# Four graph layers on one core: in layer 1, a constant one in the place of the last feature carries a term of the attention logits

## The reference

```python
x = layernorm(x + L0(x, adj))      # relational graph convolution
x = layernorm(x + L1(x, adj))      # the layer of this change
x = layernorm(x + L2(x, adj))      # attention with 8 heads
x = layernorm(x + L3(x, adj))      # graph attention with 8 heads

def L1(feat, adj):
    h = feat @ W
    Ax, Ay = h @ a_1, h @ a_2
    A_xy = (h @ a_12) @ h.T
    logits = Ax.T + Ay + A_xy
    e = where(adj > 0, leaky_relu(logits, 0.2), -9e15)
    h_prime = softmax(e) @ feat
    return elu(feat @ W_1 + h_prime @ W_2)
```

## Time and profile before

| | us |
|---|---|
| median of 3 runs | 802.0 |
| the 3 runs | 802.0, 802.37, 793.09 |
| the profiled execution, device time | 794.29 |
| its span, first to last instruction | 792.5 |
| mean granted TensorE clock | 0.976 of full |

### The profile page before, as it was taken

The page is one execution under the profiler, slowest core; times in us unless marked ns, Lnnn a source line. Parts: engine busy times, 40 slices in busy tenths (PEclk is TensorE's granted clock), DMA queues, the critical chain, the costliest instruction groups (busy, mean ns, idle before and its releaser), DMA issues.

```text
span 792.5 us, 17776 instructions
## 1 busy us (share of the span) xinstructions
PE 706.9 (89%) x6465; PEld 524.9 (66%) x6525; DVE 614.9 (78%) x1578; ACT 540.0 (68%) x933; POOL 449.6 (57%) x486
## 2 busy tenths in 40 slices
PE   3899599999678999999999999889999999999982
PEld 2777377777545666666666666667777777777761
DVE  3799648888846777878787878788888888888882
ACT  0545267777727666766666666558989898988882
POOL 5377403443334445665655566556666777677776
PEclk9999899999959999999999999999999999999997
DMA  8900000000000000000000000000000000000001
GB/s 239 247 2 1 1 1 1 2 1 2 1 0 1 2 1 2 1 2 2 1 2 1 2 1 2 2 2 1 15 15 14 15 29 15 14 16 19 24 14 41
DMA packets 28888, 14.94 MB, mean 19 GB/s; under 512 B 1920, under 2 KB 28800, under 8 KB 28800
## 3 DMA queue, kind: packets, MB, share of 16 engines
q1 hardware_dynamic: 25344, 12.59, 5.8%
q10 hardware_dynamic: 3456, 1.20, 0.7%
HBM read 9.59 MB, written 4.19 MB: 17 GB/s over the span
## 4 chain that ended last, share of the span: by engine, by line
PE 48%; issue 22%; POOL 12%; DVE 9%; POOLq 6%; ACT 2%; DVEq 0%; ACTq 0%
PE pair L954 18%; PE pair L1030 10%; POOL X L503 8%; POOLq L498 6%; PE pair L1055 4%; PE pair L1117 3%; DVE arena L932 2%; DVE nmx L938 2%; PE pair L1107 2%; PE pair L1093 2%; PE pair L1072 2%; PE pair L1104 2%; PE pair L1077 2%; PE pair L1086 2%; PE pair L1147 1%
## 5 line engine op out<-in xcount | busy, mean ns | idle before, releaser
L585 POOL TENSOR_TENSOR arena<-arena,nmx 128x1024 f32<-128x1024 f32 x64 | 121.4, 1897 | 116.2 <-DVE nmx L896 116.2
L599 POOL TENSOR_TENSOR arena<-arena,nmx 128x1024 f32<-128x1024 f32 x64 | 121.4, 1897 | 75.3 <-DVE nmx L938 75.1
L954 PE MATMUL pair<-identf,arena 128*128 128x128 f32 x1088 | 149.5, 279 | 2.5 <-ACT arena L732 2.1
L954 PEld LDWEIGHTS pair<-identf,arena 128*128 128x128 f32 x1088 | 117.5, 141 | 43.1 <-issue 38.9
L497 POOL TENSOR_TENSOR ln<-ln,neghalf 128x4 f32<-128x4 f32 x64 | 66.3, 1036 | 134.9 <-DVE ln L537 134.9
L503 POOL TENSOR_SCALAR X<-yb,ln 128x128 f32<-128x128 f32 x256 | 112.6, 453 | 11.9 <-issue 11.9
L888 DVE TENSOR_TENSOR arena<-pair,mask 128x1024 f32<-128x1024 f32 x64 | 78.4, 1225 | 51.8 <-PE pair L1030 51.7
L728 ACT COPY arena<-pair 128x1024 f32<-128x1024 f32 x64 | 64.8, 1012 | 74.0 <-PE pair L954 74.0
L1030 PE MATMUL pair<-arena,hg 32*128 32x256 f32 x512 | 91.1, 432 | 3.5 <-DVE arena L888 2.4
L757 ACT ACTIVATE arena<-pair 128x1024 f32<-128x1024 f32 x64 | 66.2, 1034 | 30.6 <-PE pair L1107 30.6
L896 DVE TENSOR_REDUCE nmx<-arena 128x8 f32<-128x1024 f32 x64 | 78.0, 1219 | 1.8
(11 more groups left out here) (169 smaller groups left out, 1405.0 us busy)
## 6 DMA issues: line engine op xcount, KB each, us to landing
X<-in_x SPq DMA_DIRECT2D x16, 256.0 KB, 6.0
arena<-in_adj SPq DMA_DIRECT2D x16, 256.0 KB, 6.2
out<-X SPq DMA_DIRECT2D x16, 256.0 KB, 2.3
nat_all<-in_L_gnn_W ACTq DMA_DIRECT2D x2, 64.0 KB, 4.5
w<-in_L_gnn_W ACTq DMA_DIRECT2D x2, 64.0 KB, 5.1
nat_all<-in_L_gnn_W_loop ACTq DMA_DIRECT2D x1, 64.0 KB, 2.7
nat_all<-in_L_gnn_Wg_loop ACTq DMA_DIRECT2D x1, 64.0 KB, 3.4
hg_bias<-in_L_gnn_b_loop ACTq DMA_DIRECT2D x1, 64.0 KB, 5.0
```

Source lines behind the costliest of these rows:

```text
L585: nc.gpsimd.tensor_tensor(v3(P2[t % 3], HEADS), v3(P2[t % 3], HEADS), nmx2[t % 2][:].unsqueeze(2).broadcast_to([128, HEADS, N]), ALU.add)\
L599: nc.gpsimd.tensor_tensor(v3(p, HEADS), v3(p, HEADS), nmx2[(t - 1) % 2][:].unsqueeze(2).broadcast_to([128, HEADS, N]), ALU.add)\
L954: last = nc.tensor.transpose(dst[:, cols(i)], src[:, cols(i)], identf[:])
```

## The change

On GpSimd a constant matrix `center` is set (the identity, with minus one in its last row, and a last column of zeros). On TensorE `w1T` is a matmul with `center` in place of a transpose, and two new products make `w12c` from `w12`. `bil` is made in two pieces: 127 columns as before, and a last column W times a_2, the vector that was spread into `wa2` before. `wa2` is gone. TensorE waits for `pool_ready` ahead of the products and no longer behind them. On VectorE two memsets, of 32 partitions by 512 columns each, write ones into the last partitions of both `xT` tiles ahead of layer 1; the copy to `xT` then writes 127 partitions, so that the last stays one. The first copy waits for the memsets. In each turn the four matmuls of line 1002 go, and `xw` uses `w12c`.

```diff
+        center = sb("center", [128, 128])
...
+        w12c = sb("w12c", [128, 2 * D])
...
-        wa2 = sb("wa2", [128, 128])
...
-        w1_at = add(w1T[:], nat["L1_gnn_W"])
+        w1_at = add(w1T[:], nat["L1_gnn_W"], center[:])
+        for half in range(2):
+            add(w12c[:, cols(half)], center[:], w12[:, cols(half)])
...
-        add(bil[:], w1T[:], a12w[:], a12w_at)
+        add(bil[:, 0:D - 1], w1T[:], a12w[:, 0:D - 1], a12w_at)
+        add(bil[:, D - 1:D], w1T[:], a_cols[:, 1:2], w1_at)
...
-        add(wa2[:], w1T[:], a_cols[:, 1:2].broadcast_to([128, 128]), w1_at)
...
-                o = bank[4 + i % 4][:, 0:128]
+                o = bank[4 + i % 4][:, 0:dst.shape[-1]]
...
+            nc.gpsimd.memset(center[:], 0.0)
...
+            select(center[:], [[0, 128]], 1 - D, fill=-1.0)
+            select(center[:], [[-1, 128]], 0)
+            select(center[:], [[1, 128]], 2 - 2 * D, fill=0.0)
             nc.gpsimd.memset(ep[:], 0.0).then_inc(sem("pool_ready"), 1)
...
             general_dve(dve)
+            for s in range(2):
+                nc.vector.memset(xT[s][96:128, :], 1.0).then_inc(sem("ones_row"), 1)
...
-                    nc.vector.tensor_copy(xT[1 - s][:], bank[0]).then_inc(sem("L1_xT"), 1)
+                    if b == -1:
+                        dve.wait_ge(sem("ones_row"), 2)
+                    nc.vector.tensor_copy(xT[1 - s][0:D - 1, :], bank[0][0:D - 1, :]).then_inc(sem("L1_xT"), 1)
...
             pe.wait_ge(sem("params"), sems["n_params"])
+            pe.wait_ge(sem("pool_ready"), 1)
             prep_pe(pe, range(first, len(prep)))
-            pe.wait_ge(sem("pool_ready"), 1)
             general_pe(pe)
...
-                        last = mm(bank[3 + 2 * (g // 2)][:, cols(g % 2, 2 * D)], xT[s][:, cols(g)], w12[:], start=True, stop=True)
+                        last = mm(bank[3 + 2 * (g // 2)][:, cols(g % 2, 2 * D)], xT[s][:, cols(g)], w12c[:], start=True, stop=True)
...
                     mm(bank[2], identb[:], mask1[:, bass.ts(b, W)], start=True, stop=False)
-                    for g in range(G):
-                        mm(bank[2][:, cols(g)], xT[s][:, cols(g)], wa2[:], start=False, stop=False)
```

## The result

| | before | changed |
|---|---|---|
| median of 20 runs | 798.08 us | 804.45 us |
| lowest to highest | 792.96 to 806.78 | 799.68 to 809.86 |
| profiled execution, device time | 794.29 us | 806.01 us |
| span, mean granted clock | 792.5 us, 0.976 | 804.3 us, 0.955 |

The ratio is 1.0082, with a 95% interval of 1.0059 to 1.0105: the change costs 6.4 us by the medians. That is inside the range and within 2%, but 16 times the +0.4 us of my sum. The 802.4 us came near 804.45 only because the three runs that I built on lay high; with the median of 20 the same sum would have said 798.5.

A forecast was written before the change was run, and what follows sets the result against it. A 7.23 us circle through ScalarE, TensorE and VectorE was taken to bound layer 1's turns. Preparation +0.45, memsets +1.0 and first turn -1.1 made about +0.4 us on 802.0, so 802.4 us, range 791 to 805.

The forecast's parts named there:

- my sum: Whole kernel: preparation +0.45, memsets +1.0 and first turn -1.1 us make +0.35, say +0.4 us; bounds -2 to +3 us.
- The circle: Layer 1 turns: z, elu, exponentials, transposes and copy across engines set the 7.23 us turn; line 1002 lies outside, gain zero.
- TensorE bounds the turns after all: Rival, layer 1: 0.90 us saved in each of 15 turns, 12 us won, 790 us from the median; chance 0.06.
- The first turn: First turn of layer 1: nothing covers line 1002, so removing it gains 1.1 us; bounds 0.9 and 1.8.
- two signs that I had named: Before layer 1: last preparation copy ends 0.3 to 0.6 us later; first copy to xT starts near 96.4, not 94.95.
- my three terms: Start of layer 1: preparation +0.45 us, memsets +1.0 us, removal in the first turn -1.1 us, together +0.35 us.
- The memsets: VectorE ahead of the first copy to xT: two memsets and 0.1 us of wait cost +1.0 us; bounds 0.6 and 1.9.
- Preparation: TensorE's products ahead of layer 1: 19 in place of 17, 2 x 0.23 = +0.45 us; bounds 0.2 and 0.9.
- Covered: Kernel's first microseconds: setting center on GpSimd costs nothing, at most 1.2 us without cover; the moved wait is also free.
- The clock at the start: Head of layer 1: its later start against TensorE's clock rise may move the time by +-1.7 us.
- The clock falls inside layer 1: Rival, layer 1 turns: idle of 1.51 us drops the clock, 18 us lost, 820 us from the median; chance 0.04.
- The level of the forecast: Base for the whole kernel: median of three timed runs, 802.0 us; one run at 793.1, two at 802.

The follow-up runs named there:

- e2: Kernel before, with the four matmuls of line 1002 left out of every turn and nothing else changed; ratio 1.0039 to the kernel before.
- e8: Changed kernel, with the last turn of layer 1 put between the second and third of layer 2's four first steps; ratio 1.0067 to the kernel before.
- e1: Changed kernel, with four matmuls shaped like the removed ones put back in every turn of layer 1, their result unread; ratio 1.0112 to the kernel before.
- e5: Kernel before, plus two one-column memsets of an unread tile on VectorE ahead of layer 1 and the wait for them; ratio 1.0085.
- e11: Kernel before, with layer 1's last turn moved early into layer 2's first steps and filling matmuls in TensorE's waits at the passage; 787.3 us, ratio 0.9885.
- e12: Changed kernel, with layer 1's last turn moved early and filling matmuls at the passage, four in the last batch's turn; 789.3 us, ratio 0.9898 to the kernel before.
- e6: Changed kernel, plus four one-column memsets on VectorE behind the two memsets of the ones; ratio 1.0061 to the kernel before.
- e10: Changed kernel, plus four one-column memsets on VectorE and four unread matmuls shaped like the removed ones in every layer 1 turn; ratio 1.0054 to the kernel before.
- e4: Changed kernel, with filling matmuls into an unread PSUM bank in TensorE's waits at the passage from layer 1 to 2; ratio 1.0085 to the kernel before.
- e7: Kernel before, with the last turn of layer 1 put between the second and third of layer 2's four first steps; ratio 1.0025.

## Why the prediction was right or wrong, point by point

**The circle (right).** The turn is 7.23 us, and the idle is 27.0 us in all, 1.50 a turn. The rival "TensorE bounds the turns after all" is out. The busy share of 89% was indeed no guide.

**The first turn, -1.1 us (right).** e2 has -1.2 us at the same clock. The changed kernel's first exponential:

```profile
108.91 0.40 ACT L689 ACTIVATE loopm<-work,nm 128x128 f32<-128x128 f32 x1
```

It is 1.85 us later than in the earlier trace rows, not 0.35. 0.7 us of that stand before layer 1 begins. For the rest, the preparation lies in a stretch of half clock in this execution, at 83 to 90 us, where the kernel before had full; that is the clock again. So two signs that I had named did not come: the last preparation copy ends at 91.56 us, 3.1 us later and not 0.3 to 0.6, and the first copy to `xT` starts at 98.80 and not near 96.4. The trace of e8 is a fairer pair, with half clock ahead of the first exponential only from 92.4 to 102.6 us (91.6 to 101.8 before). From GpSimd's start on the last batch but one of layer 0 to the first exponential it is 20.6 us in e8 and 20.7 before: 0.1 us less, where my three terms make 0.35 more.

**The memsets, +1.0 us (right).** VectorE's timeline:

```profile
97.67 1.03 DVE L831 MEMSET xT<- 32x512 f32 x2 [1.02 <-issue]
98.80 0.69 DVE L850 COPY xT<-pair 127x512 f32<-127x512 f32 x1
```

98.80 - 97.67 = 1.13 us, with 0.1 us for the wait. My sum from the memset of 1024 columns had 1.0. The estimate by the rate in VectorE: DVE Perf Modes of the Trainium skill (Zero memsets can be issued as uint32), 0.15 us higher, came nearer.

**Preparation, +0.45 us (not measured alone).** e1, which keeps the work of line 1002, is at +1.3 us at the same clock, for preparation and memsets together, where the sum has 1.45.

**"Covered" (wrong, by a few tenths of a microsecond).** I put the work on `center` at nothing. GpSimd is busy with its constants until 13.97 us in place of 12.35, 1.35 us of it with the selects of `center`, and two copies of VectorE beside that now take 0.82 us where they took 0.35:

```profile
13.23 0.82 DVE L799 COPY bias<-bias_part 1x256 bf16<-1x256 bf16 x2
```

```profile
13.18 0.35 DVE L792 COPY bias<-bias_part 1x256 bf16<-1x256 bf16 x2
```

The second line is that of the kernel before. TensorE waits for the chain in which these copies stand, at the start of layer 0. GpSimd first scales in layer 0 at 30.27 to 31.05 us in the eight traces with the change's set-up and at 29.33 to 30.11 in the six without it, on average 0.8 us apart. About half of that is already there at TensorE's first matmul, which waits for a DMA; whether the change has a part in this no run shows.

**The sum, +0.4 us (right at the same clock, in part by luck).** The changed kernel has +0.4 us there. But the start of layer 1 costs less than my terms, and the head of the kernel, which I had at nothing, makes up for it.

**The clock (wrong; this step failed).** "*The clock at the start* ... I take +-1.7 us for it" looked for the clock only at the head of layer 1, and the rival "The clock falls inside layer 1" only in its turns, where it is at 1.00. The term that decides is at the passage to layer 2, which my text didn't price at all. I had "moved by as much" for the layers behind. In its place the runs show a loss of mean clock from 0.971 to 0.959, 7 us. Two memsets, which put a stall of 0.36 us at VectorE's last residual, bring such a loss alone (e5); an early last turn with fillers that hold the clock removes it (e11, e12).

**The level of the forecast (wrong).** I took 802.0 as the base since two of three runs lay there; of 20 the median is 798.08. I wrote that the profile doesn't tell what parts the runs. It is the clock: at 0.978 the kernel before takes 793.0 us, at 0.969 some 797.5, and the one execution at 0.957 took 806.7.

**Still open.** Why the changed kernel keeps a lower clock when the stall is moved (e6, e10), and how much of e2's lower clock is real. Why the kernel before itself, without any edit, falls in levels from 793 to 807 us. What the stall is made of was not tried; that it moves with the number of instructions on VectorE is shown, no more.

## What to carry to other kernels

Where a stage ends with TensorE waiting and the next begins sparsely, look at the granted clock there before and after any edit, also of an edit far away: here 0.1 us of instructions on VectorE were worth 6 to 7 us. Plot each execution's time over its mean clock; the distance from that line gives the cost of an edit to a few tenths of a microsecond where the medians scatter by five. Work that fills TensorE's waits at such a passage, with VectorE's late step moved into an earlier wait, gained 1.1%; neither the fillers of e4 nor the early step of e7 and e8 did so alone.

## What the hardware showed that I had not expected

- TensorE worked almost without a gap from 240 to 258 us, on transposes, score matmuls of 32 rows and value matmuls, and the clock stayed at half; in the changed kernel, e1, e5 and e10 it came back only by the second batch's V products, 23 to 26 us behind the 235.0 of the kernel before.
- Between elu and residual VectorE stalls for 0.36 us at one place of its stream: at the sixth batch in the kernel before, at the last with two instructions more, and at neither of the two with six. It goes by multiples of 256 of VectorE's records.
- The kernel before falls into levels: of 82 executions, 32 lie at 792.6 to 794.3 us, 7 at 795.1 to 796.4, 34 at 797.1 to 799.5 and 9 above 800.
